# Loading a broadcast table chunk by chunk over all 128 partitions instead of by 32 partitions with four chunks each

## The reference

```python
e = jnp.stack([tbl_0[ids[:, 0]], ..., tbl_31[ids[:, 31]]], axis=1)   # [1024, 32, 16]
x0 = xk = e
for W in (W0, W1, W2):                # [32, 32, 64], [32, 64, 64], [32, 64, 64]
    xk = relu(einsum('bmd,bhd,mhk->bkd', x0, xk, W))
    outs.append(sum(xk, axis=2))
z = concatenate(outs, axis=1)         # [1024, 192]
h = concatenate([z, dense_ctx], axis=1)
h = maximum(h @ W_top1 + b_top1, 0)
h = maximum(h @ W_top2 + b_top2, 0)
y = h @ W_top3
```

## Time and profile before

| | |
|---|---|
| median of 3 runs | 631.96 us (630.64 to 633.41) |
| the profiled execution | 630.55 us |
| its span, first to last instruction | 628.7 us |
| mean granted TensorE clock | 0.984 of full speed |
| PE busy | 594.6 us |
| DVE busy | 585.8 us |
| POOL busy | 443.2 us |
| ACT busy | 355.5 us |
| moved by the DMA engines | 119.82 MB |

### The profile page before, as it was taken

How to read it: one execution, slowest core, us unless ns; L and a number is a source line. 1 busy time by engine, 2 the same in 40 slices (tenths; PEclk the granted TensorE clock), 3 DMA queues, 4 the chain that set the end, 5 groups by cost and what they waited for, 6 DMA issues and landing times.

```text
span 628.7 us, 8924 instructions
## 1 busy us (share of the span) xinstructions
PE 594.6 (95%) x3046; PEld 243.0 (39%) x3046; DVE 585.8 (93%) x398; ACT 355.5 (57%) x665; POOL 443.2 (70%) x305
## 2 busy tenths in 40 slices
PE   4398998999999999999999999999999999999988
PEld 4252332234343354334443354334443354334434
DVE  4759999999999989999999999999999999999873
ACT  0173754729394663829385574829385674829361
POOL 5767887888888884988878887988878460806120
PEclk9579999999999999999999999999999999999999
DMA  6899989994997689695999779795999789690000
GB/s 176 192 236 271 210 249 210 274 211 113 252 264 183 137 248 214 205 218 128 238 218 246 154 231 213 230 217 129 221 216 258 155 247 217 212 213 17 2 0 1
DMA packets 60175, 119.82 MB, mean 191 GB/s; under 512 B 15271, under 2 KB 33734, under 8 KB 60054
## 3 DMA queue, kind: packets, MB, share of 16 engines
q1 hardware_dynamic: 49414, 114.69, 73.7%
q0 software_dynamic: 7584, 1.96, 3.8%
q10 hardware_dynamic: 3152, 2.86, 1.7%
HBM read 115.27 MB, written 5.25 MB: 192 GB/s over the span
## 4 chain that ended last, share of the span: by engine, by line
PE 53%; POOL 21%; DVE 12%; issue 7%; ACT 3%; SPq 2%; DMA 1%; DVEq 0%; ACTq 0%; POOLq 0%
PE acc L968 47%; POOL emb L447 12%; POOL z_pool L472 8%; DVE z_dve L529 8%; PE psm L1071 2%; SPq L426 2%; PE psm L1079 2%; DMA x_rot<-in_tbl_dram 1%; DVE z_dve L549 1%; DVE x0b L698 1%; PE acc L983 1%; ACT xq L717 1%; ACT xq L725 1%; ACT xq L771 1%; PE psm L1086 1%
## 5 line engine op out<-in xcount | busy, mean ns | idle before, releaser
L529 DVE TENSOR_TENSOR z_dve<-xq,x0b 128x2048 f32<-128x2048 f32 x179 | 398.5, 2279 | 12.4 <-ACT xq L717 7.5
L968 PE MATMUL acc<-z_dve,w_cin 128*64 128x512 f32 x1688 | 387.2, 597 | 9.9 <-DVE z_dve L529 7.1
L472 POOL TENSOR_TENSOR z_pool<-x0b,xs 128x2048 f32<-128x2048 f32 x45 | 205.3, 4565 | 89.4 <-ACT xs L717 88.9
L447 POOL DMA_INDIRECT emb<-in_tbl_dram,ids_all x224 | 218.3, 974 | 66.3 <-issue 61.3
L968 PEld LDWEIGHTS acc<-z_dve,w_cin 128*64 128x64 f32 x1688 | 127.3, 136 | 230.5 <-issue 166.9
L754 ACT ACTIVATE xq<-acc 64x512 f32<-64x512 f32 x64 | 36.5, 570 | 123.1 <-PE acc L968 122.4
L968 PE MATMUL acc<-z_pool,w_cin 128*64 128x512 f32 x360 | 85.0, 593 | 1.4 <-POOL z_pool L472 1.3
L549 DVE TENSOR_TENSOR z_dve<-xq,x0b 128x1024 f32<-128x1024 f32 x64 | 75.8, 1215 | 6.9 <-ACT xq L754 5.0
L717 ACT ACTIVATE xs<-acc 64x512 f32<-64x512 f32 x124 | 73.4, 592 | 1.7
L771 ACT ACTIVATE xq<-acc 32x512 f32<-32x512 f32 x128 | 72.2, 564 | 1.9
L725 ACT ACTIVATE xq<-acc 32x512 f32<-32x512 f32 x128 | 72.2, 564 | 1.7
(11 more groups left out here) (99 smaller groups left out, 241.8 us busy)
## 6 DMA issues: line engine op xcount, KB each, us to landing
x0b<-x0t SPq DMA_DIRECT2D x120, 512.0 KB, 13.2
x_rot<-x0t SPq DMA_DIRECT2D x60, 512.0 KB
x_rep<-x0t SPq DMA_DIRECT2D x15, 512.0 KB, 7.9
x0b<-x0t SPq DMA_DIRECT2D x16, 256.0 KB, 8.1
emb<-in_tbl_dram,ids_all POOLq DMA_INDIRECT x224
x0t<-emb_t SPq DMA_DIRECT2D x28, 128.0 KB
w_cin<-in_L_rec_W_dram SPq DMA_DIRECT2D x16, 64.0 KB
x_lo<-x0t SPq DMA_DIRECT2D x15, 64.0 KB
```

The costliest lines, as they stand in the source:

```text
L447: nc.gpsimd.indirect_dma_start(out=rows[:, D * f:D * f + D], out_offset=None, in_=tables[f], in_offset=bass.IndirectOffsetOnAxis(ap=ids_al ...
L472: nc.gpsimd.tensor_tensor(z_pool[:, n % ZP_SLOTS, :, :], x0b[b % 2][:, 2 * j:2 * j + 2, :], xs[l - 1][:, :].unsqueeze(1).broadcast_to([P, ...
L529: nc.vector.tensor_tensor(z_dve[:, base % Z_SLOTS, :, :], in0.unsqueeze(1).broadcast_to([P, 2, N]), in1, ALU.mult).then_inc(z_made, 1)
L968: ins = nc.tensor.matmul(acc[l][K * side:K * side + K, :], weights[c], z[:, c, NH * side:NH * side + NH], start=start and c == 0, stop=sto ...
```

## The change

`load_x0b` now issues one transfer for each chunk, onto all 128 partitions: the source pattern is four rows (one for each r), each repeated 32 times. Before, it issued one for each r, onto 32 partitions and all chunks c0 to c1: one row repeated 32 times for each chunk. With four chunks a call, both make four transfers of 512 KB. In the first tile, with two chunks a call, 4 x 256 KB become 2 x 512 KB, and the threshold in `x0b_ready` follows. Nothing else is changed; what lands in `x0b` is the same.

```diff
@@ -321,9 +321,7 @@
         def x0b_ready(t, s, j):
-
-            first = 2 * 4 * 16 if s == 0 else 4 * 16
-            return x0b_in[s][j // 2], 4 * 16 * t + first
+            return x0b_in[s][j // 2], 4 * 16 * (t + 1)
@@ -367,9 +365,8 @@
             def load_x0b(t, s, c0, c1):
-                for r in range(4):
-                    sp.dma_start(x0b[s][Q * r:Q * r + Q, c0:c1, :],
-                                 x0_rows(t, s, r + 4 * c0, [[0, Q], [4 * ROW, c1 - c0], [1, N]])
+                for c in range(c0, c1):
+                    sp.dma_start(x0b[s][:, c, :], x0_rows(t, s, 4 * c, [[ROW, 4], [0, Q], [1, N]])
                                  ).then_inc(x0b_in[s][c0 // (CH // 2)], 16)
```

## The result

| | before | changed |
|---|---|---|
| median | 632.68 us (6 runs) | 913.84 us (912.08 to 914.89, 6 runs) |
| ratio | | 1.446, 95% interval 1.443 to 1.450 |
| span of the profiled execution | 628.7 us | 912.1 us |
| mean granted TensorE clock | 0.984 | 0.856 |

Of the six runs of the kernel before, four took 630.6 to 633.4 us and two, which the ratio leaves out and no trace explains, 1038.6 and 1038.8 us.

What follows compares the result with a forecast made beforehand. DVE and PE bound the kernel before; changed, four DMA engines' queue would. Block 1's table at 120.7, 7 tiles of 101.3, 42.5 to the end, 4 for half clock and 1.85 outside the span give 878 us, range 835 to 1490.

Steps and rivals of the forecast that it cites:

- What bounds the kernel before: DVE and PE share the pace; x0b's load is hidden, cover some 38 us for 20 us, 18 us of slack.
- Part (1): x0b's transfers: both sides are cut in the same number of parts, so four engines carry all of x0b.
- Part (2): x0b's rate: four engines at 25.1 GB/s each take 41.8 us a block; with other traffic a block takes 49.3 us.
- Part (3): SP's wait for the x0t writes before load_l0: queues empty 2.7 us a tile, so a tile takes 101.3 us.
- (4): The start: block 0's x0b table lands at 72.0 us, block 1's at 120.7 us.
- (5): The sum: 120.7, 7 tiles of 101.3, 42.5 to the end, 4 for half clock, 1.85 outside the span: 878 us.
- The signs: SP's queue near 47750 packets, DMA share 0.3 to 0.5, DVE waiting 15 us a block, x0b issued every 50 us.
- Sixteen engines: Rival: x0b dealt by the destination alone, 10.5 us instead of 20, all in slack; 632 us within 1; chance 0.10.
- Something between the rates: Rival: four engines at 18 GB/s, 58.3 us for an x0b table, some 1120 us; chance 0.17.
- the lasting half rate: Rival: four engines in step on shared SBUF ways, 13.2 GB/s each, x0b 79.4 us a block, 1480 us; chance 0.20.

Runs made afterwards that it cites:

- The two runs that took a disturbance away: Changed kernel with x_rot's transfers cut to 16 of 1024 columns: 828.3 us; changed kernel with x0t writes issued between the halves of a tile's odd table: 915.8 us.
- The two engines at 55 GB/s: Kernel before, from the second tile on each x0b chunk in two transfers of 64 partitions, each from 2 rows 32 times: 1419.8 us, single run.

## Why the prediction was right, and where it was off

**What bounds the kernel before: right.** The table was hidden with a cover of 38 us for 20, and 16 engines on 128 partitions, which load it faster, change nothing (ratio 1.003).

**Part (1), four engines: right, and shown.** The dealing by both sides' outermost counts was taken from 125 rows on 5 engines; source counts of 2, 4, 8 and 32 give 2, 4, 8 and 16 engines by the packets. Only the source's count was varied: the destination's was 32, 64 or 128 in every run, so what a small count there does is not shown. The Trainium skill, "DMA: Bandwidth & Descriptors", section "Rules for kernel authors", lets an outermost count under 16 use at most that many engines. The traces agree: 48518, 47750 and 47846 packets are those of 8, 4 and 2 engines.

**Part (2), the rate: right in kind, low by 4%.** Where SP's queue is the only one that moves anything, each engine moves 104 / 4 = 26.0 GB/s, not 25.1:

```profile
336.00:340.00 4.00, 0.00 (x0) 0.00 (x0) 0.00 (x0) 0.00 (x0) 0.00 (x0) 0.95 0.25 104
```

At 26.0 a table takes 40.3 us and not 41.8; the work of a tile is 95.2 us and not 98.6. (The 26.6 of two expectations counts the gathers as well.)

**Part (3), waits: the term that was mis-sized.** It had 2.7 us a tile beyond the work. Measured are 106.4 - 95.2 = 11.2. The stretches of the changed kernel account for most: the empty queue 3 us (as predicted); 8 us of `load_l0` at 339 GB/s, 21.2 for each engine instead of 26.0, lose 1.5; 7 us behind it, in which SP's queue moves 0.61 MB, 87 GB/s instead of 104, lose 1.1; some 10 us of the other `load_l0`, with 2.24 MB on SP's queue, 14 GB/s for each engine, lose 4.6. The rest, about 1 us, I can't place. Two errors partly cancel: 3.4 us too much work, 8.5 too little disturbance, 5.1 us a tile. The two runs that took a disturbance away gave back 2.7 us and 0.7, so these losses seem to replace each other and aren't a simple sum.

**Parts (4) and (5).** Block 1's table landed at 125.5, not 120.7 (+4.8); 7 tiles gave +35.7; from the last landing to the end 41.8 us instead of 46.5 (-4.7). The clock was indeed low around that landing, a mean of 0.58 granted from 868 to 872 and of 0.56 from 872 to 876, but nothing of the 4 us allowed for it shows: the tail is as long as the 42.5 us before. 876.3 + 4.8 + 35.7 - 4.7 = 912.1, the measured span. That the total came within 4% of the forecast owes something to luck, since the errors partly cancel; the mechanism does not.

**The signs.** The packets came as forecast, to the packet. DVE waited 280.8 / 16 = 17.6 us a block (15 forecast), and SP issued a table every 53 us (50 forecast).

**The rivals.** Sixteen engines did not come. Something between the rates and the lasting half rate did not come either, though short stretches with slower engines did: that rival had the right place and the wrong duration. (By its own terms 18 GB/s gives 1142 us, where the prediction has some 1120.) The Trainium skill, "SBUF — State Buffer", section "Door 1: The DMA port swizzle", puts partition p + 32 on the port of p, and has partitions 0 to 31 reach half of the ports. The old form's 211 GB/s, half of 396 to 407, agrees. The two engines at 55 GB/s show no cost of sharing a port; where they stood to each other no row tells.

**What stays open:** why 16 engines on 128 partitions run at 407 GB/s at one time and at 228 to 313 at another, the same pattern among them. The gathers' share of the engines' time, 1 to 23% by stretch, explains a part at most: it is 2.8% where the rate is 228. That engines which meet on the same partitions' ways slow each other, and drift in and out of it, would fit; no run sets the phase between engines by itself.

## What to carry to other kernels

Before a transfer's pattern is rearranged, look at the outermost count on both sides (only the source's was varied here): it decides over how many DMA engines the transfer is dealt, and a broadcast written as "4 rows, each 32 times" gets 4 where "one row, 32 times" gets 16. The packet count of the queue tells the number: all the counts above come out if each engine reports each transfer once. And a hidden load is judged by the most loaded engine's work against the block, not by the mean share of all: here 27.4 us of work on each of eight engines, against a block of 35.7 us, still cost 0.6%, and 47.6 us on each of four cost 45%.

## What the runs showed that was not expected

- The share of busy engines does not tell whether they move at full rate: 1.02 to 1.04 stands beside 211, 228, 339 and 407 GB/s. A share with its GB/s gives the rate of an engine that is busy, 13 to 25 here, and 26 where few are.
- SP is held up by its queue: eight issues took 22 to 34 us on four engines and 55 to 69 us on two (part of SP's timeline in that run below), against 4 to 7 before. What stands behind them in the program is late by that, on engines that are idle.

```profile
362.90 62.89 SPq L372 DMA_DIRECT2D x0b<-x0t  x8
```

- Taking away the empty queue of 3 us a tile gave 0.7 us a tile (915.8 us in all), while the transfer that filled it ran slower beside the others.
- A transfer onto 32 partitions moved 211 GB/s with one row repeated and with 32 different rows alike.
